# A conditioned Mamba-2 block on one core: opening without padding products, transposes on row halves, the dt series moved

## The reference, cut to what matters

```
att = softmax(MLP(cond));  w = att . bank(8, 32, 32);  b = att . bias_bank
h   = w(per sequence) @ x + b                        # mixing over the 32 tokens
p   = h @ in_proj.T -> gate(4096), xBC(4096 + 2*1024), dt(64)
xBC = silu(causal conv of 4 taps);  dt = softplus(dt + bias)
state = state * exp(dt*A) + dt*x (x) B;  y = state . C + D*x    # 64 heads of 64, 8 groups
x   = x + (rmsnorm(y) * silu(gate)) @ out_proj.T
x   = x + masked dense(grouped conv of 9 taps(x))    # mask from softmax(x3 @ centroids)
```

## Time and profile before

| | |
|---|---|
| median of three runs | 1627.02 us |
| the profiled execution | 1627.06 us |
| its span, first to last instruction | 1625.3 us |
| TensorE busy | 1604.8 us, 99% |
| weight loads busy | 1299.1 us, 80% |
| VectorE | 1059.1 us, 65% |
| ScalarE | 845.9 us, 52% |
| GpSimd | 773.4 us, 48% |

### The profile page before, as it was taken

How to read it: one execution, slowest core, us unless ns; L and a number is a source line. 1 busy time by engine, 2 the same in 40 slices (tenths; PEclk the granted TensorE clock), 3 DMA queues, 4 the chain that set the end, 5 groups by cost and what they waited for, 6 DMA issues and landing times. The chain is left out here.

```text
span 1625.3 us, 31516 instructions
## 1 busy us (share of the span) xinstructions
PE 1604.8 (99%) x12495; PEld 1299.1 (80%) x12495; DVE 1059.1 (65%) x1741; ACT 845.9 (52%) x1372; POOL 773.4 (48%) x731
## 2 busy tenths in 40 slices
PE   9999999999999999999999999999999999999997
PEld 6778888888888888887787888888888888887665
DVE  6876666565656576676686656565667656565455
ACT  4654546555555545565554555555555556544321
POOL 3564644545453645454255554646364545534203
PEclk9999999999999999999999999999999999999999
DMA  5111102011111101011112201111110201116772
GB/s 190 59 53 33 41 20 66 27 53 40 40 53 34 59 16 58 21 53 40 33 41 73 65 28 53 41 40 53 34 59 8 66 21 53 41 36 153 181 156 104
DMA packets 50290, 93.08 MB, mean 57 GB/s; under 512 B 5664, under 2 KB 6304, under 8 KB 50144
## 3 DMA queue, kind: packets, MB, share of 16 engines
q1 hardware_dynamic: 50144, 91.06, 19.6%
HBM read 82.59 MB, written 8.45 MB: 56 GB/s over the span
## 5 line engine op out<-in xcount | busy, mean ns | idle before, releaser
L487 PE MATMUL PS<-xh,wh 128*128 128x512 f32 x1280 | 518.7, 405 | 0.6 <-DVE xl L369 0.6
L487 PE MATMUL PS<-xh,wl 128*128 128x512 f32 x1280 | 500.0, 391 | 0.0
L487 PE MATMUL PS<-xl,wh 128*128 128x512 f32 x1280 | 499.8, 390 | 0.0
L522 DVE SCALAR_TENSOR_TENSOR cb<-PS,P,cb 128x496 f32<-128x496 f32 (+2 forms) x576 | 412.6, 716 | 132.5 <-ACT cb L508 119.0
L184 POOL TENSOR_TENSOR wl<-rw,wh 128x512 fp32r<-128x512 f32 x160 | 211.8, 1328 | 188.6 <-ACT wh L179 170.6
L721 POOL TENSOR_TENSOR ysum<-yq 128x256 f32<-128x256 f32 x128 | 109.4, 855 | 364.0 <-ACT yq L706 363.8
L487 PEld LDWEIGHTS PS<-xh,wl 128*128 128x128 f32 x1280 | 240.2, 188 | 52.9
L487 PEld LDWEIGHTS PS<-xh,wh 128*128 128x128 f32 x1280 | 240.5, 188 | 49.1 <-ACT wh L179 1.0
L487 PEld LDWEIGHTS PS<-xl,wh 128*128 128x128 f32 x1280 | 241.0, 188 | 44.3
L508 ACT ACTIVATE cb<-PS,P 128x512 f32<-128x512 f32 x192 | 148.4, 773 | 205.2 <-PE PS L487 205.2
L650 DVE TENSOR_TENSOR big<-Lt,gmt 128x512 f32<-128x512 f32 x128 | 102.6, 843 | 158.0 <-ACT Lt L588 158.0
(11 more groups left out here) (197 smaller groups left out, 2230.6 us busy)
## 6 DMA issues: line engine op xcount, KB each, us to landing
rw<-in_w_in SPq DMA_DIRECT2D x160, 256.0 KB, 2.7
ro<-in_w_out SPq DMA_DIRECT2D x64, 256.0 KB, 2.9
wh<-x2s SPq DMA_DIRECT2D x32, 258.5 KB, 5.2
wl<-x2s SPq DMA_DIRECT2D x32, 258.5 KB, 5.1
x2s<-acc SPq DMA_DIRECT2D x16, 260.0 KB, 5.5
out_x<-acc SPq DMA_DIRECT2D x16, 256.0 KB, 2.3
acc<-in_x SPq DMA_DIRECT2D x3, 1024.0 KB, 9.4
acc<-in_x SPq DMA_DIRECT2D x4, 256.0 KB, 4.8
```

Source lines behind the costliest of these rows:

```text
L487: fn = lambda e, k=k, w=w, v=v, i=i: e.matmul(PS[:, bank, :], w[:, m, 128 * k:128 * k + 128], v[:, k, a:a + 512], start=(i == 0), stop=(i ...
L522: dve.op(lambda e, d=d, w=w: e.scalar_tensor_tensor(out=cv[:, :, d:32], in0=pv[:, :, 0:32 - d], scalar=w, in1=cv[:, :, d:32], op0=ALU.mult ...
```

## The change

The opening loses the padding products between the mixing tiles and four of the six before them; the vector part of tiles 1 and 2 stands ahead of the first mixing tile, and the dt weights are split after the four tiles. The transposes of two tiles are issued together, each cut into two of 64 rows (the two heads of the slice), whose results go to two banks; VectorE reads both banks. The banks are numbered anew. The series gets 6 steps in slot 9 and 7 in slot 4, and the turn of blocks 1 to 3 moves from the end of slot 6 to the end of slot 5.

```diff
-        PP, PT, PG, PY, PO = (0, 1, 4), 2, 3, (5, 6), (7, 7, 5, 6)
-        SEG = (7, 6)
-        TB = (PT, PO[2], PT, PO[0])
+        PP, PT, PG, PY, PO = (0, 1, 2), 6, 3, (4, 5), (7, 7, 5, 4)
+        SEG = (7, 4)
+        TB = ((PO[2], PT), (PT, PO[0]))
...
-        def A(n, i):
+        def A(n, r):
+            if r == 0:
+                for m in range(6):
+                    pe.wait("silu", (n, m))
                 if n == 0:
                     pe.wait("dre", (0, 1))
+                    pe.wait("xl", 7)
+                else:
+                    pe.wait("dtx", (n - 1, 3))
+                    pe.wait("acc", (n - 1, 2))
...
             else:
+                pe.wait("dtx", (n, 1))
                 pe.wait("L", (n, 0))
...
+            for i in (0, 1):
+                a = 128 * (2 * r + i)
+                for j in range(4):
+                    for v in (0, 1):
+                        p, c = slice(64 * v, 64 * v + 64), 256 * i + 64 * j
+                        fn = lambda e, j=j, v=v, a=a, p=p, c=c: e.transpose(PS[:, TB[r][v], c:c + 64], xs[p, j, a:a + 128],
+                                                                         ident[p, 64 * v:64 * v + 64])
...
-                dtx[:, r, :].rearrange("p (h c) -> p h c", h=8), PS[:, TB[i], :].rearrange("p (h c) -> p h c", h=8),
+                dtx[:, r, :].rearrange("p (j v c) -> p j v c", j=4, v=2),
+                PS[:, b0:b0 + 2, 256 * r:256 * r + 256].rearrange("p v (j c) -> p j v c", j=4),
...
         mixing_weights_part(1, 4)
-        keep_busy(6)
+        keep_busy(2)
         X_dve(1)
+        X_dve(2)
         for T in range(4):
             X_pe(T, [("mx", 1)] if T else [("sx", 0)])
-            keep_busy((4, 1, 1, 0)[T])
             if T == 0:
-                X_split(0)
-                X_dve(2)
-                split_w_hi(0, 0)
-            if T == 1:
                 X_dve(3)
-                dt_weights()
-            if T >= 1:
-                X_split(T)
-                split_w_hi(0, T)
+            X_split(T)
+            split_w_hi(0, T)
+        dt_weights()
...
-        pace0 = (0, 3, 2, 3, 2, 3, 0, 0, 0, 3)
-        pace = (0, 0, 0, 0, 5, 5, 0, 0, 0, 3)
+        pace0 = (0, 3, 3, 3, 3, 1, 0, 0, 0, 6)
+        pace = (0, 0, 0, 0, 7, 0, 0, 0, 0, 6)
...
+                if n - 1 in block_at and m == 5:
+                    assert not chain
+                    DT_pe(block_at[n - 1], [("acc", (n - 1, 1))])
+                    DT_split(block_at[n - 1])
                 if m == 7:
                     A(n, 0)
-                    A(n, 1)
...
                 if m == 9:
-                    A(n, 2)
-                    A(n, 3)
+                    A(n, 1)
```

More of the change, by code:

```diff
@@ L577, in seg @@
                 else:
-                    pe.wait("xl", 5 + r)
+                    pe.wait("xl", 5 + 2 * r)
                 pe.op(lambda e, r=r: e.matmul(PS[:, SEG[r], :], uf[:, :], avh[:, 512 * r:512 * r + 512], start=True, stop=False))
@@ L588, in expo @@
                 act.op(lambda e, r=r: e.activation(Lt[:, 512 * r:512 * r + 512], PS[:, SEG[r], :], ACT.Exp), "L", (n, r))
-        def A(n, i):
[L591 to L594, removed]
+        def A(n, r):
+            if r == 0:
+                for m in range(6):
+                    pe.wait("silu", (n, m))
                 if n == 0:
                     pe.wait("dre", (0, 1))
-                elif n in block_at:
-                    pe.wait("xl", 4 * block_at[n] + 3)
[L599 to L606, removed]
+                    pe.wait("xl", 7)
+                else:
+                    pe.wait("dtx", (n - 1, 3))
+                    pe.wait("acc", (n - 1, 2))
+                if n in block_at and n >= 1:
+                    pe.wait("xl", 4 * block_at[n] + 3)
             else:
+                pe.wait("dtx", (n, 1))
                 pe.wait("L", (n, 0))
-            for j in range(4):
-                fn = lambda e, j=j: e.transpose(PS[:, TB[i], 128 * j:128 * j + 128], xs[:, j, a:a + 128], ident)
-                pe.op(fn, "T", (n, i)) if j == 3 else pe.op(fn)
+                if n in block_at:
+                    pe.wait("dre", (block_at[n], 1))
+            for i in (0, 1):
[5 more added lines that the diff above has]
+                                                                         ident[p, 64 * v:64 * v + 64])
+                        pe.op(fn, "T", (n, 2 * r + 1)) if (i, j, v) == (1, 3, 1) else pe.op(fn)
         def G_all(n):
@@ L636, in A_dve @@
             z, r = 4 * n + i, i % 2
-            dve.wait("T", (n, i))
+            b0 = TB[i // 2][0]
+            dve.wait("T", (n, i | 1))
             dve.wait("dtt", 2 * half + tb)
@@ L641, in A_dve @@
             dve.op(lambda e: e.tensor_tensor(
-                dtx[:, r, :].rearrange("p (h c) -> p h c", h=8), PS[:, TB[i], :].rearrange("p (h c) -> p h c", h=8),
-                bc(dtt[:, 4 * tb + i, 8 * g:8 * g + 8].rearrange("p (h o) -> p h o", o=1), 128, 8, 64), ALU.mult), "dtx", (n, i))
+                dtx[:, r, :].rearrange("p (j v c) -> p j v c", j=4, v=2),
+                PS[:, b0:b0 + 2, 256 * r:256 * r + 256].rearrange("p v (j c) -> p j v c", j=4),
+                bc(dtt[:, 4 * tb + i, 8 * g:8 * g + 8].rearrange("p (j v o) -> p j v o", j=4, v=2), 128, 4, 2, 64), ALU.mult), "dtx", (n, i))
         def M_dve(n, i):
@@ L868, in stage @@
                     G_mask(n)
-                turned_now = n == 0 or n - 1 in block_at
-                if m == 6 and not turned_now:
+                if n >= 1 and m == 6:
                     av(n)
@@ L889, in stage @@
                 evac(n, m)
-                if m == 6 and turned_now:
-                    t = block_at[n - 1] if n else 0
+                if n == 0 and m == 6:
                     assert not chain
-                    DT_pe(t, [("acc", (n - 1, 1)) if n else ("xl", 5)])
-                    DT_split(t)
-                    av(n)
+                    DT_pe(0, [("xl", 5)])
+                    DT_split(0)
+                    av(0)
                 if n == 0 and m < 6:
@@ L943, in stage @@
                     if b is not None:
-                        D_pe(b, [("dtx", (n, 0))])
+                        D_pe(b, [("dtx", (n, 1))])
                         chain.extend(D_chain(b))
                 if m == 9:
-                    A(n, 2)
-                    A(n, 3)
+                    A(n, 1)
                     Y(n, 0)
```

## The result

The changed kernel takes 1629.28 us, the median of 20 runs (1626.85 to 1632.74); the kernel before, run beside it, 1627.01 (20 runs). One of those 20 took 2058.78 us, a slow run that the ratio leaves out. The ratio is 1.0014, 95% interval 1.0008 to 1.002: slower by 0.14%, where 0.4% faster was forecast. The profiled execution took 1629.26 us, its span is 1627.5, so 2.2 us more than before on either count.

The account below looks back on a forecast made before the run. TensorE's issued work plus few stalls was taken to bound the 32 stages. Terms -2.3 (slot 7), -1.1 (slot 9), -3.8 (turn), +1.9 (series), -1.2 (opening) sum to -6.5: 1627.06 to 1620.6 us; range 1616.5 to 1628.

Parts of the forecast that it names:

- The opening: Before the stages: with padding products gone, tile 3's buffer is asked for earlier and VectorE starts earlier; -1.2 us, bounds -3 to +1.
- so the weights are ready at 29.0: Opening: mixing weights of T=4 come 1.2 us earlier, as weight tile 3 lands at 22.0 and ScalarE starts at 22.1.
- The late clock: Rival, opening: the clock stays low through tiles 1 to 3 and projection 0; +2.5 instead of -1.2, 1624.3 us; chance 0.05.
- the stall at the turn of stage 0 stay: Stage 0: TensorE's stalls at the turn and segment sums stay, only moved by 1.2 us.
- The turn: Stages 1 and 17: moved from slot 6 to slot 5, it loses its waits and those of the segment sums; -3.8 us.
- the bank order and its wait (acc of tile 1) are the same: Turn of dt in slot 5: bank order and the wait for acc of tile 1 stay the same; part of the -3.8 term.
- The waits of the segment sums: Stages 1 and 17: these go once the series is finished in slot 4; 2.6 us of the -3.8.
- The series eats what it frees: Rival, slots 9 and 4 of stages with a turn: contended steps triple, seven stand ahead of slot 4's taps; 1625.8 us; chance 0.15.
- The out-product of tile 0: Stages 1, 16, 17: three more series steps in slot 9 delay the first y and this product; +1.9 us, bounds 0 to +4.
- overlap as forecast: Slots 7 and 9: two row halves of a transpose work side by side, a pair taking 0.058 us.
- no cost from the new wait in slot 9: Slot 9: waiting for the first exponential before both tiles costs 0, as Y would start at 478.58, before 478.74.
- Slot 7: Sixteen half transposes replace eight whole ones: 1.27 against 1.34 us, 0.07 less per stage, 2.3 us over 32 stages.

Follow-up runs that it names:

- opening_only: Kernel before with the new opening alone (2 padding products, none between the tiles, vector part of tile 2 ahead); 1629.84 us, ratio 1.0018.
- pad_ahead: Changed kernel with six padding products ahead of tile 0 again, none between the tiles; 1626.37 us, ratio 0.9997.
- padded: Changed kernel with the padding back at both places (6 ahead of tile 0, then 4, 1, 1 between the tiles); 1626.90 us, ratio 1.0002.
- turn_slot6: Changed kernel's row halves and series paces with the opening of before and the turn in its old slot 6; 1623.75 us (one run).
- turn_other_bank: Changed kernel with the opening of before; in stages 1 and 17 the turn writes to the first transposed tile's bank; 1624.06 us, ratio 0.9977.
- series_only: Kernel before with the new places of the series and of the turn (slot 5) alone; 1628.75 us, ratio 1.0014.

## Why the prediction was wrong

**The opening failed, -1.2 against +1.7.** The step was "so the weights are ready at 29.0". It took the durations of TensorE at the full clock from before and removed work ahead of the rise. The late clock was among the rivals, with its place (tiles 1 to 3 and the start of projection 0) and a price of +2.5; the runs show +1.7 in after, where the clock was up and fell, and +2.6 in opening_only, where it came late. It was given 0.05, far too little for a change that took away four of the six products behind which the clock rose (it was still at the lower level in these six and at the full one in the eight products of tile 0): that row was read for the time it would free. The term also had the stall at the turn of stage 0 stay; it shrank by 0.45 us, so the opening alone cost more than the +1.7. The mechanism put in the forecast, a buffer and GpSimd's weights, is there in pad_ahead, but brings 0.55 us and not 1.2: ScalarE had its tile at 22.60 and not at 22.1 (22.17 to 23.07 in padded, turn_slot6 and turn_other_bank, where it waited for the DMA too).

**The turn failed, -3.8 against -0.2.** The step was "the bank order and its wait (acc of tile 1) are the same". The wait is the same in the code, but a slot earlier acc of tile 1 isn't there yet: before, it was issued at 102.13 for a turn at 105.89; after, it is issued at 105.51 for a turn that could start at 104.98. The seven steps ahead of it in slot 4 push it by 1.7 beyond the shift of the opening. The waits of the segment sums went, as forecast (2.6). In their place came S with 0.7, and the turn's own wait grew from 1.1 to 2.9. turn_other_bank, with the same series and another bank for the turn, gives 2.8 us back in stages 1 and 17. "The series eats what it frees" named the seven steps of slot 4 rightly and looked for who waits at projection 7; it is acc of tile 1, and by it the bank.

**The out-product of tile 0**: +1.9 forecast, 2.5 measured (0.42, 1.24 and 0.88), inside its bounds; without the halves, in series_only, 2.0 (0.25, 1.04 and 0.67). Stage 17 has the same slack and was cheap by 0.3.

**The halves**: overlap as forecast, pairs at 0.065 for 0.058, no cost from the new wait in slot 9. Slot 7 gave 0.044 a stage for 0.07 (1.4 us for 2.3), slot 9 about 1 us in the late stages for 1.1. The difference of 0.02 in a block of 1.3 is a sum of six small readings; times 32 it is 0.9 us.

**Sum.** Forecast -6.5, measured +2.2: 8.7 apart, of which the turn 3.6, the opening 2.9, the out-product 0.6. The 1.6 that are left are put down to the halves; part of it is that they have fewer late stages to gain in once the segment sums don't wait, and the split of this rest was not measured. The sign came from the first two, and both were waits or states that the change itself moved.

## What to carry to other kernels

A product of constants is not wasted if the clock rises in it or behind it: before removing it, recost all that follows at the lower level, and treat that as the forecast until a row shows other work that raises the clock. Profiles of one opening differed by 2 us with the state in which they began: look at the first rows of both before comparing marks. When a step moves up a slot, look up when each event it waits for is issued, not only the one the move is about; the bank's last reader can be the later one. On an engine with one list and a contended neighbour, steps moved elsewhere delay what stands next there: six of them in slot 9 cost 2.5 us at one out-product, and three of these put to slot 2 instead cost 1.2 us at the next, twice.

## What the runs showed of the hardware

- In opening_only TensorE worked through four mixing tiles (12.3 to 24.6 us) and four constant products at the lower level, and the spacing fell to 0.23 only within the first projection, at 27.5. The column of the clock read 1.00 all the while, since no change had been recorded before: the group time of eight products, 2.07 or 1.16, tells the level.
- The clock can fall again behind a single wait: behind 1.50 us in padded seven products were 0.43 apart, behind 3.07 in turn_other_bank twelve. Behind 1.11 us in pad_ahead and 1.08 in turn_slot6 none were.
- A series step of 0.42 us takes 1.47 beside a GpSimd product of 1.30 in after, and 1.34 to 1.54 in the other kernels. The Trainium skill (SBUF — State Buffer, SBUF: two separate sides) says that such operations of VectorE and GpSimd exclude one another for the whole instruction. The rows nearly agree: the other operation still runs 763.16 - 761.97 = 1.19 us, and with the 0.42 that gives 1.61, where 1.47 was measured.
